# One output array for all scatters of an expert layer, each issued after the one in front has landed

## The reference, cut to what matters

```python
def _L0_ffn_ref(x, ln_g, ln_b, rW, rb, W1, b1, W2, b2):
    z = _layernorm(x, ln_g, ln_b)
    probs = jax.nn.softmax(jnp.einsum('bth,he->bte', z, rW) + rb, axis=-1)
    topv, topi = jax.lax.top_k(probs, 2)
    mask = jnp.sum(jax.nn.one_hot(topi, 8) * topv[..., None], axis=-2)
    w = mask / jnp.maximum(jnp.sum(mask, axis=-1, keepdims=True), 1e-08)
    hid = jax.nn.gelu(jnp.einsum('bth,ehf->btef', z, W1) + b1, approximate=False)
    outs = jnp.einsum('btef,efh->bteh', hid, W2) + b2
    return x + jnp.sum(outs * w[..., None], axis=2)
...
x = x + _L0_xattn_ref(...)
x = x + _L0_ffn_ref(_layernorm(x, axis=-1), ...)
```

## Time and profile before

| | |
|---|---|
| median of 3 runs | 916.51 us (916.13 to 918.11) |
| span of the profiled execution | 916.6 us |
| PE busy / DVE busy / POOL busy | 783.3 / 670.5 / 546.1 us of the span |
| attention and routing | up to about 660 us |
| the 57 expert tiles | first scatter issued at 674.8, last at 892.1 us |
| final sum of the two arrays | issued at 895.1 us, 18.8 us to landing |

### The profile page before, as it was taken

One profiled execution on the slowest core, in us unless ns is written; L12 is line 12 of the kernel. 1 busy time (PEld: TensorE's weight loads), 2 busy tenths in 40 slices (PEclk: granted clock), 3 DMA queues, 4 the chain that ended last, 5 costly groups with the idle time before them and its releaser, 6 DMA issues. The chain is left out here.

```text
span 916.6 us, 26602 instructions
## 1 busy us (share of the span) xinstructions
PE 783.3 (85%) x8118; PEld 613.9 (67%) x8119; DVE 670.5 (73%) x1879; ACT 510.4 (56%) x1351; POOL 546.1 (60%) x609
## 2 busy tenths in 40 slices
PE   3549799999999999999999987518699999999970
PEld 1326477777777777777776654418699888888960
DVE  1439799999999999999998887564756565565640
ACT  2226488888888888888887755410143333333420
POOL 2322577787868777777776653330156666667750
PEclk9779899999999999999999987755599999999995
DMA  8575366757676766667677863454034343434437
GB/s 184 128 164 126 80 148 142 172 140 167 137 167 138 163 142 156 146 152 157 142 163 175 205 147 106 113 122 165 11 60 65 60 62 63 65 59 65 70 40 143
DMA packets 156687, 112.51 MB, mean 123 GB/s; under 512 B 68322, under 2 KB 150386, under 8 KB 156114
## 3 DMA queue, kind: packets, MB, share of 16 engines
q1 hardware_dynamic: 134396, 81.51, 39.3%
q0 software_dynamic: 11360, 17.37, 11.7%
q10 hardware_dynamic: 10886, 13.06, 5.0%
HBM read 39.99 MB, written 23.88 MB: 70 GB/s over the span
## 5 line engine op out<-in xcount | busy, mean ns | idle before, releaser
L932 DVE TENSOR_REDUCE negmax<-s_row 100x1 f32<-100x361 f32 x512 | 251.3, 523 | 36.1 <-PE s_row L613 28.9
L776 ACT ACTIVATE p_t<-s_t 128x400 f32<-128x400 f32 x384 | 188.8, 502 | 70.9 <-PE s_t L632 62.5
L613 PE MATMUL s_row<-k_stack,q_stack 125*128 125x361 bf16 x512 | 134.5, 326 | 25.4 <-DMA k_stack<-pad_rows 10.7
L632 PE MATMUL s_t<-q_stack,k_stack 128*128 128x100 bf16 x1536 | 129.0, 211 | 13.0 <-DMA q_stack<-m_part 7.6
L632 PEld LDWEIGHTS s_t<-q_stack,k_stack 128*128 128x128 bf16 x1536 | 93.3, 99 | 60.7 <-issue 26.7
L1196 PE MATMUL p_h<-zgt,w_k 128*128 128x128 f32 x912 | 115.9, 281 | 3.2 <-DVE w_k L1383 3.2
L1242 ACT ACTIVATE hidt<-p_h,b_k 128x128 f32<-128x128 f32 x228 | 65.2, 369 | 88.1 <-PE p_h L1196 81.2
L1196 PEld LDWEIGHTS p_h<-zgt,w_k 128*128 128x128 f32 x912 | 107.9, 194 | 7.5 <-issue 5.3
L599 PE MATMUL pj<-wv_s,ct 128*128 128x256 f32 x384 | 109.1, 408 | 0.0
L1205 PE MATMUL p_y<-k_stack,hidt 128*128 x456 | 107.7, 379 | 0.0
L937 DVE TENSOR_SCALAR p_t<-p_t 128x1200 f32<-128x1200 f32 x128 | 100.1, 782 | 4.5 <-ACT p_t L776 4.4
(11 more groups left out here) (178 smaller groups left out, 1371.8 us busy)
## 6 DMA issues: line engine op xcount, KB each, us to landing
k_stack<-k_part SPq DMA_DIRECT2D x192, 192.0 KB, 3.6
q_stack<-q_part SPq DMA_DIRECT2D x192, 64.0 KB, 2.0
ct<-in_ctx_t SPq DMA_DIRECT2D x32, 361.0 KB, 4.7
w_s<-in_w ACTq DMA_DIRECT2D x8, 512.0 KB, 4.6
k_stack<-in_w ACTq DMA_DIRECT2D x8, 512.0 KB, 5.4
zscr<-zn SPq DMA_DIRECT2D x32, 100.0 KB
z_in<-zscr SPq DMA_DIRECT2D x32, 100.0 KB
zf_d<-zf_s SPq DMA_DIRECT2D x32, 100.0 KB
```

Of the source, the lines that this page charges most:

```text
L613: nc.tensor.matmul(s_row[h % 2][:, 0:KEYS], q_stack[0:MROW, b.slot, h, :], k_stack[0:MROW, b.slot, h, 0:KEYS], start=True, stop=True).then ...
L632: last = nc.tensor.matmul(s_t[g % 2][:, j * Q:j * Q + Q], k_stack[:, b.slot, h, kt * 128:kt * 128 + 128], q_stack[:, b.slot, h, 0:Q], star ...
L776: nc.scalar.activation(p_t[:, quad % 2, kt, :], s_t[g % 2][:, 0:4 * Q], ACT.Exp).then_inc(exp_done, 1)
L932: v.tensor_reduce(negmax[:, b.slot, h:h + 1], s_row[h % 2][0:Q, 0:KEYS], AXIS.X, ALU.max, negate=True).then_inc(max_done, 1)
```

## The change

All scatters add to `out`. Before each scatter but the first, POOL waits until the scatter in front has landed: a constant in the steps that are written out, a register (`landed`, two of them, starting at 32 and raised by 16) in the loop. The fill with zeros on POOL, its spread to `odd_d` on SP, the wait for that spread and the final sum are gone, with the array itself.

```diff
             @blk.sync
             def _(sp):
                 sp.dma_start(b1_s[:], b1).then_inc(b1_loaded, 16)
-                sp.wait_ge(zeros_ready, 1)
-                sp.dma_start(odd_d.rearrange("b q d -> (b q d)").rearrange("(p r n) -> p r n", p=128, n=640),
-                             zeros[:].unsqueeze(1).broadcast_to([128, B * Q * D // (128 * 640), 640])).then_inc(odd_zeroed, 16)
                 store_gates(sp, 1)
...
             @blk.gpsimd
             def _(pool):
-                nc.gpsimd.memset(zeros[:], 0.0).then_inc(zeros_ready, 1)
...
+                landed = [pool.alloc_register(f"landed{k}") for k in range(2)]
+                pool.reg_mov(landed[0], 32)
+                pool.reg_mov(landed[1], 32)
...
                 pool.wait_ge(x2_stored, 16 * B)
-                pool.wait_ge(odd_zeroed, 16)
+
+                def after_scatter_before(k):
+
+                    if k.known:
+                        after(pool, scattered[1 - k.slot], 16 * ((k.index + 1) // 2))
+                        return
+                    pool.wait_ge(scattered[1 - k.slot], landed[k.slot])
+                    pool.reg_add(landed[k.slot], landed[k.slot], 16)
...
                     pool.wait_ge(y_ready, k.index + 1 if k.known else scatters[k.slot])
                     pool.reg_add(scatters[1 - k.slot], scatters[k.slot], 1)
-                    pool.indirect_dma_start((out_rows, odd_rows)[k.slot], bass.IndirectOffsetOnAxis(idx_s[:, k.slot:k.slot + 1], 0), ys[:, k.slot, :], None,
+                    after_scatter_before(k)
+                    pool.indirect_dma_start(out_rows, bass.IndirectOffsetOnAxis(idx_s[:, k.slot:k.slot + 1], 0), ys[:, k.slot, :], None,
                                             bounds_check=B * Q - 1, oob_is_err=False, compute_op=ALU.add).then_inc(scattered[k.slot], 16)
...
                 for s in range(2):
                     pool.wait_ge(scattered[s], 16 * len(range(s, NT, 2)))
-                wide = [t.rearrange("b q d -> (b q d)").rearrange("(r n) -> r n", n=2048) for t in (out, odd_d)]
-                pool.dma_start(wide[0], wide[1], accum_op=ALU.add, max_dma_last_dim=8192).then_inc(odd_added, 16)
-                pool.wait_ge(odd_added, 16)
```

More of the change, by code:

```diff
@@ L127, in build @@
 def build(nc, x, ctx_t, wq_t, bq, wk_t, bk, wv_t, bv, gamma, beta, ln_g, ln_b, rw, rb, w1, b1, w2, b2,
-          ident_d, route_c, sum_c, zscr, zf_d, odd_d, out):
+          ident_d, route_c, sum_c, zscr, zf_d, out):
     es = ExitStack()
@@ L202, in build @@
         LATE = B - EARLY
-        w2_loaded, cst_loaded, odd_zeroed = sem("w2_loaded"), sem("cst_loaded"), sem("odd_zeroed")
+        w2_loaded, cst_loaded = sem("w2_loaded"), sem("cst_loaded")
         gates_ready, gates_stored = sem("gates_ready"), sem("gates_stored")
@@ L1108, in build @@
             w1_k = sb(ffn, "w1_k", [128, 2, 2, HF])
-            zeros = sb(ffn, "zeros", [128, 640])
             zgt = sb(ffn, "zgt", [128, 2, 2 * 128])
@@ L1124, in build @@
             scattered = [sem(f"scattered{k}") for k in range(2)]
-            zeros_ready, odd_added = sem("zeros_ready"), sem("odd_added")
             zgt_done, zgt_copied, up_done, b1_ready, gelu_done = (sem(k) for k in ("zgt_done", "zgt_copied", "up_done", "b1_ready", "gelu_done"))
@@ L1262, in _ @@
                 pool.reg_mov(scatters[0], 1)
+                landed = [pool.alloc_register(f"landed{k}") for k in range(2)]
+                pool.reg_mov(landed[0], 32)
+                pool.reg_mov(landed[1], 32)
                 zf_rows = zf_d.rearrange("b q d -> (b q) d")
                 out_rows = out.rearrange("b q d -> (b q) d")
-                odd_rows = odd_d.rearrange("b q d -> (b q) d")
                 def gather(k):
@@ L1466 @@
     args["zf_d"] = nc.dram_tensor("zf_d", [B, Q, ROW], FP32, kind="Internal").ap()
-    args["odd_d"] = nc.dram_tensor("odd_d", [B, Q, D], FP32, kind="Internal").ap()
     args["out"] = nc.dram_tensor("out_x", [B, Q, D], FP32, kind="ExternalOutput").ap()
```

## The result

The changed kernel takes 939.7 us (median of 4 runs, 938.15 to 942.19) where the kernel before takes 916.3 (4 runs, 913.83 to 918.11). The ratio is 1.026, with a 95% interval of 1.023 to 1.028: **slower by 2.6%**, as forecast, and 23.4 us in the medians against 26.5 forecast. The profiled execution has a span of 936.4 us, in a run of 938.15.

What follows compares the result with a forecast made beforehand. PE was taken to set the pace before (3.88 us per tile), the chain of scatter landings after (4.68). 916.6 - 19.1 + 44.8 + 1.2 = 943.5 us, said as 943; 934 to 953 should hold 8 times in 10.

Steps and rivals of the forecast that it cites:

- The sum gone: After the last scatter's landing: the final sum of the two arrays, with nothing beside it, goes whole, -19.1 us.
- The wait: Between scatters in the tiles: a step becomes landing plus wake-up, 4.68 instead of 3.88 us, 56 times, +44.8 us.
- the last dispatch: Before the last scatter: its issue takes 1.96 instead of 0.72 us again, +1.2 us once.
- The landing: Each scatter from start to landing: 3.81 us for a full tile; 2.68 for the last, which holds no rows.
- The wake-up: On POOL, from a landing to the next scatter's start: 0.87 us, through wait, register step and dispatch.
- The choice between 0.29 and 0.87: POOL's wake-up: 0.87 forecast; at 0.29 the step is 4.10 us, the time 909.8. Rival that the chain doesn't bind: 0.08.
- The gather hidden in the wait: On POOL behind each scatter: the following tile's gather, 1.07 us, ends before the landing and costs nothing.
- The zeros: Before the tiles: POOL's fill and SP's DMA of zeros go; they were over long before the first scatter, gain nothing.
- before the change PE sets the pace, with a little lost at the turns of the loop: In the tiles before the change: PE's own work of 3.74 us bounds the pace of 3.88 us per tile.
- PE's share: In the tiles after the change: PE busy near 80%, standing still 0.94 us of each 4.68 us.
- The clock: Rival in the tiles: PE, pausing more, falls to 1.2 GHz half of the time, about 956 us; chance 0.05.
- the 897 us that follow: From the skill page's fit: a landing of 2.3 us, a step of 3.2, PE still the bound, time near 897.

Runs made afterwards that it cites:

- e2: The kernel before without the final sum of the two arrays; 897.91 us, ratio 0.980, 18.2 us less.
- e1: The kernel before with each scatter also waiting for the landing of the one in front, two arrays, zeros and sum kept; 960.95 us, ratio 1.050.
- e6: The changed kernel with POOL issuing the following tile's gather behind the wait for the landing instead of ahead of it; 1023.2 us (one run).
- e3: The changed kernel with the fill, spread and wait for zeros of a second array put back; 941.98 us beside 939.7 without them.
- e5: The kernel before with two of the four matmuls of the second product left out; 913.1 us (one run) beside 916.85.
- e12: The kernel before with all matmuls but without DVE's two gate instructions from tile 4 on; 907.9 us beside 918.3, ratio 0.990.
- e4: The changed kernel with two of the four matmuls of the second product left out; 941.35 us beside 939.7.
- e7: The changed kernel with scatters that overwrite instead of adding; 897.7 us (one run).
- e8: The changed kernel with scatters of only the first 64 of each tile's 128 rows; 909.5 us (one run).
- e9: The changed kernel waiting only where the expert changes, by a table read behind the data wait; full waits in first tiles and last six; 911.5 us, ratio 0.995.
- e10: e9 with the table read ahead of the gather and used up to tile 55; 902.4 us beside 918.3 for the kernel before, ratio 0.983.

## Why the prediction was right, point by point

- **The sum gone, -19.1 us.** Right; 18.2 measured (e2).
- **The wait, +46.0 us in all (44.8, and 1.2 for the last dispatch).** Right in its mechanism and size: 44.9 (e1). The landing was taken from two tiles at the end as 3.81; it is 3.8 in the median over all. The wake-up was taken from scatters that waited for DVE, 0.87; behind a landing it is 0.88 in the rows above. The choice between 0.29 and 0.87 decided the sign, and the structure of the instruction (a register step and a dispatch behind the wait) was what to choose by. The last dispatch again took long, 1.75 us of issue. Such a long one was not seen at the end only: one step in the loop has 1.49 us of issue (at 840.73), and its step is 5.59 us; the same tile had the longest step before, 4.85.
- **The gather hidden in the wait.** Right, shown from the other side by e6.
- **The zeros, nothing.** Right: the times leave up to 2 us open, the traces show none (e3).
- **The sum of the parts.** The profile's own span came out at 936.4 against 943.5. Of the 7.1 us, 5.2 lie ahead of the first scatter, in the attention, where the two executions differed before any changed instruction; 1.8 are the 56 steps (261.5 us instead of 263.3). Most landings take 3.7 to 3.9 us, but four in the chain take 3.0 to 3.3, presumably those of tiles with few rows, which the sum did not have. The closing 5.3 us are as forecast. Against the medians (23.4 us instead of 26.5) an increase of 26.7 from e1 and e2 remains nearer to the forecast than the changed kernel itself; about 3 us of that are not accounted for in the times; the zeros were the one candidate that was tried, and the traces show nothing for them.
- **Span and time.** The prediction set the span of 916.6 equal to the median of 916.51. In the profile after, the run's time is 1.75 us longer than the span. So the profiled execution of before was probably one of the longer ones. It moved the forecast by less than 2 us.
- **Wrong: "before the change PE sets the pace, with a little lost at the turns of the loop".** The time forecast didn't hang on it, since the step of 3.88 was read and not worked out. But e5's forecast did, and fell. The 3.97 us of the loop are DVE's program with its gaps; PE's 3.74 stands close behind, POOL's 3.27 next. The step that failed was to take the engine with the highest busy share, and a work sum near the step, for the bound, and to call the rest loss. PE was busy 98% of the time and still didn't bind: its first products take 1.84 to 2.05 us in the loop's chain and 1.79 in e12. Of the rest, the turn of the loop is one part: DVE's gap before `idx_s` is 1.1 us once in four tiles and 0.6 to 0.7 in the others. The two rows that the 3.74 came from lie ahead of the loop's slow part.
- **PE's share.** 80% was forecast, 86% is in the row. The 3.74 us were made of products that had not waited. In the changed kernel nearly each first product waits for its weights, and then takes 2.05 us instead of 1.79:

```profile
736.51 2.05 PE L1191 MATMUL p_h<-zgt,w_k 128*128 128x128 f32 x16 [0.37 <-DVE w_k L1384]
```

  With it a tile is 2.05 + 1.73 + 0.22 = 4.0 us of PE, 86% of 4.67.
- **The clock.** The rival didn't occur: 1.00 from 674 to 884 us, with PE busy 86%. Nor did the clock cost anything in e4.
- **The Trainium skill's page "DMA: Bandwidth & Descriptors".** The estimate of 2.3 us from it fits none of the adding scatters (2.7 us with no rows, 3.8 with 128), and the 897 us that follow didn't come. It fits the scatter that overwrites: one landing of e7 took 2.29 us, and the time was 897.7.

## What to carry to other kernels

A wait for the DMA in front turns overlapped transfers into a chain, and its step is not the landing alone but landing plus wake-up of the issuing engine; here 3.8 us hid under a pace of 3.88 and 4.67 didn't, so the 0.88 us from landing to next start, which cost nothing before, made the change lose. Compare a chain's step with the pace to well under a microsecond, times the number of steps, before trading it for a single saving at the end. The engine with the highest busy share need not be the one that sets the pace; follow the chain through the loop, and cut one engine's work at a time to see. And where order is only needed between some pairs, wait only there, and read what decides it ahead of the wait.

## What the runs showed of the hardware

- An adding scatter of 1 KB rows lands 2.7 us after its start with no rows, 3.1 to 3.2 with 64 (e8), 3.8 with 128. One behind the other to the same array (after) or alternating between two (e1) made no difference. Overwriting instead of adding cut the issue on POOL from 1.58 to 1.02 us and one landing from 3.71 to 2.29 us (e7).
- Reading one number from memory into a register costs its engine a gap: on POOL it made the wake-up 1.76 us where it stood behind the wait (e9) and 1.02 with the read ahead (e10), on DVE it is part of a gap of 0.3 to 1.1 us of "issue" twice per tile (before). A busy share of 59% was a full engine here.
- PE's granted clock was 1.00 in the changed kernel with PE busy 113.86 of 132 us. In e4 it stayed at 1.00 between 710 and 842 us with PE busy 94.89 of 132, and was 0.96 in the next 42 us, with one fall to 0.50 at 851 to 854. In e6 it was 0.94 with PE busy 94.81 of 132: there a round takes 6.1 us and PE waits about 2 us in each, and the clock fell in five of some 21 rounds (a first product of 3.44 us in such a round, 2.05 in the others). The fall in e4 moved no time (the step there was 4.7 us like the others); for e6 it stays open, since the profile's chain begins only at 979 us.

```profile
710.00:842.00 132.00, 94.89 (x628) 76.20 (x629) 65.11 (x257) 42.91 (x141) 75.61 (x58) 1.00 0.34 54
...
710.00:842.00 132.00, 94.81 (x551) 79.51 (x549) 49.43 (x195) 32.40 (x107) 60.74 (x44) 0.94 0.26 41
...
749.82 0.64 PE L1179 MATMUL p_zt<-ident,zg 128*128 128x128 f32 x2 [2.25 <-DMA zg<-zf_d,idx_g]
750.26 3.44 PE L1191 MATMUL p_h<-zgt,w_k 128*128 128x128 f32 x16
```

The first row is of e4, the others are of e6. The Trainium skill, "TensorE: Matmul & The Clock Gate", section "HAM oscillation — how this bites in real kernels", tells of a kernel in which TensorE waited for a DMA in each round of a loop, for longer than here, and fell to the low clock in every round. e6 is such a loop and agrees in part, with falls in some rounds; in the changed kernel's loop, with shorter pauses, there was none.
